# Expert loop: the down product of the preceding tile moved behind both gate and up pairs, the output copy behind both silus

## What is computed

```python
logits = x_flat @ gate_w.T
top_v, top_i = jax.lax.top_k(logits, 2)          # 2 of 8 experts for each token
hidden = silu(x_flat @ wge.T) * (x_flat @ wue.T)  # 512 hidden features
acc + we[:, None] * (hidden @ wde.T)
...
x = x + 0.5 * ffn(layernorm(x))
x = x + mamba(ln(x)) + mamba_reversed(ln(x))
x = x + 0.5 * ffn(layernorm(x))
```

## Time and profile before

| | us |
|---|---|
| median of 3 runs | 2637.85 (2635.95 to 2637.89) |
| span of the profiled execution | 2637.8 |
| PE, DVE, POOL, ACT busy | 2244.2, 2254.8, 2198.0, 1909.6 |
| the two expert loops in it | some 123 to 495 and 2222 to 2593 |

### The profile page before, as it was taken

The page is one execution under the profiler, slowest core; times in us unless marked ns, Lnnn a source line. Parts: engine busy times, 40 slices in busy tenths (PEclk is TensorE's granted clock), DMA queues, the critical chain, the costliest instruction groups (busy, mean ns, idle before and its releaser), DMA issues.

```text
span 2637.8 us, 49017 instructions
## 1 busy us (share of the span) xinstructions
PE 2244.2 (85%) x15840; PEld 1920.7 (73%) x15840; DVE 2254.8 (85%) x3430; ACT 1909.6 (72%) x3628; POOL 2198.0 (83%) x1402
## 2 busy tenths in 40 slices
PE   4899999768888898898898898988988768999992
PEld 3799999547676677777777676766777647999982
DVE  8766666789999999999999999999999897666666
ACT  4355555378998998998999899999898544555551
POOL 3577777369999999999999999999999936777771
PEclk8899999889999999999999999999999878999996
DMA  7011111433333333333333333333333240111116
GB/s 247 17 48 50 49 49 49 121 107 104 105 109 106 109 102 101 106 107 100 109 103 102 110 103 105 110 106 106 105 102 111 76 160 25 49 50 49 49 50 204
DMA packets 156813, 248.60 MB, mean 94 GB/s; under 512 B 22082, under 2 KB 66018, under 8 KB 155874
## 3 DMA queue, kind: packets, MB, share of 16 engines
q1 hardware_dynamic: 137568, 202.79, 25.9%
q0 software_dynamic: 18208, 37.26, 5.2%
q10 hardware_dynamic: 866, 6.43, 0.6%
HBM read 213.10 MB, written 33.29 MB: 93 GB/s over the span
## 4 chain that ended last, share of the span: by engine, by line
POOL 28%; PE 23%; issue 22%; DVE 14%; ACT 8%; DMA 4%; POOLq 0%; ACTq 0%; DVEq 0%; SPq 0%
POOL buf L484 10%; POOL buf L545 9%; DVE buf L914 6%; PE bank L1544 6%; POOL token_outputs L494 5%; PE bank L1419 4%; DMA buf<-state_rows 3%; PE bank L1329 3%; PE bank L1519 3%; POOL buf L532 2%; DVE buf L901 2%; ACT scaled L1194 2%; ACT over L1161 2%; DVE bank L886 2%; PE bank L1348 2%
## 5 line engine op out<-in xcount | busy, mean ns | idle before, releaser
L545 POOL TENSOR_TENSOR buf<-buf 128x1024 f32<-128x1024 f32 x512 | 1199.9, 2378 | 33.8 <-PE bank L1544 28.9
L914 DVE TENSOR_TENSOR_SCAN buf<-over,bank 128x512 f32<-128x512 f32 x832 | 953.6, 1198 | 5.2 <-PE bank L1519 2.6
L1161 ACT ACTIVATE over<-wgu,negA 128x510 f32<-128x510 f32 x832 | 541.2, 710 | 39.6 <-DVE buf L914 28.5
L1544 PE MATMUL bank<-id_sb,buf 128*128 128x128 f32 x4096 | 521.8, 282 | 6.3 <-POOL buf L545 6.3
L1544 PEld LDWEIGHTS bank<-id_sb,buf 128*128 128x128 f32 x4096 | 483.9, 146 | 55.8 <-issue 46.5
L1348 PE MATMUL bank<-parts 128*128 128x256 f32 x3408 | 480.3, 291 | 3.3 <-DVE buf L764 1.9
L1348 PEld LDWEIGHTS bank<-parts 128*128 128x128 f32 x3408 | 428.8, 192 | 7.2 <-issue 4.1
L1194 ACT ACTIVATE scaled<-wd_sb,I 128x256 f32<-128x256 f32 x896 | 377.3, 498 | 22.3 <-PE bank L1519 22.2
L494 POOL DMA_INDIRECT token_outputs<-buf,slot_out x284 | 287.7, 1013 | 111.1 <-issue 83.2
L484 POOL DMA_INDIRECT buf<-token_rows,slot_token x284 | 297.1, 1046 | 95.4 <-issue 89.7
L1519 PE MATMUL bank<-id_sb,scaled 128*128 128x128 f32 x1792 | 257.2, 281 | 91.3 <-ACT scaled L1194 40.8
(11 more groups left out here) (170 smaller groups left out, 2978.0 us busy)
## 6 DMA issues: line engine op xcount, KB each, us to landing
buf<-state_rows SPq DMA_DIRECT2D x608, 256.0 KB, 3.2
token_rows<-buf SPq DMA_DIRECT2D x32, 256.0 KB, 2.3
wd_sb<-token_outputs SPq DMA_DIRECT2D x16, 512.0 KB, 4.1
buf<-token_outputs SPq DMA_DIRECT2D x16, 512.0 KB, 4.9
buf<-token_rows,slot_token POOLq DMA_INDIRECT x284, 2.6
token_outputs<-buf,slot_out POOLq DMA_INDIRECT x284, 2.3
out<-X SPq DMA_DIRECT2D x16, 256.0 KB, 3.8
wgu<-wgT ACTq DMA_DIRECT2D x1, 2048.0 KB, 8.1
```

The lines of the kernel that those rows point to most:

```text
L545: pool.tensor_tensor(hC[:, b, :].rearrange("p (c w) -> p c w", c=C), hs[:, b, :].rearrange("p (c w) -> p c w", c=C), Cs[:, b, :].unsqueeze ...
L914: V.tensor_tensor_scan(hs[:, b, w], dA[:, b, c, :, :].rearrange("p s t -> p (s t)"), source, 0.0, ALU.mult, ALU.add).then_inc(s[f"scan_don ...
L1161: ins = A.activation(dA[:, n % R, c, :, 1:], delta[r][:, c * W:(c + 1) * W].rearrange("p (s t) -> p s t", s=S)[:, :, 1:], ACT.Exp, scale=n ...
L1544: ins = M.matmul(bank[4 + q // 2][:, at:at + P], hC[:, n % R, c * W + q * P:c * W + (q + 1) * P], id_sb[:, :], is_transpose=True, start=Fa ...
```

## The change

On PE `down(i-1)` moves from between the two halves of tile i to behind `up(i,1)`. On ACT `copy_out(i-1)` moves from between the two silus to behind `silu(i,1)`. Nothing is added or taken away. It applies to every tile but the first, in both mixtures of experts.

```diff
@@ ACT, four() @@
                         silu(i, 0)
+                        silu(i, 1)
                         if not (isinstance(i, int) and i == 0):
                             copy_out(i - 1, (q - 1) % 4, k if q else k - 1)
-                        silu(i, 1)
@@ PE, four() @@
                         gate(i, q % 2, 0)
                         up(i, q % 2, 0)
+                        gate(i, q % 2, 1)
+                        up(i, q % 2, 1)
                         if not (isinstance(i, int) and i == 0):
                             down(i - 1, (q - 1) % 2, (q - 1) % 4)
-                        gate(i, q % 2, 1)
-                        up(i, q % 2, 1)
```

## The result

| | before | after |
|---|---|---|
| median of 7 runs, us | 2637.89 (2635.95 to 2639.8) | 2647.51 (2644.11 to 2649.35) |
| span of the profiled execution, us | 2637.8 | 2642.8 |
| first scatter of each loop, us behind the loop's first gather | 19.2, 19.1 | 20.2, 20.5 |
| POOL's pace, 1st to 67th scatter, us a tile | 5.355, 5.342 | 5.432, 5.367 |
| first transfer of the 67th to that of the 71st scatter, us | 16.4, 16.6 | 16.4, 16.1 |

The changed kernel is slower: ratio 1.0034, 95% interval 1.0023 to 1.0045. The medians differ by 9.6 us, the two profiled executions by 5.0: a run's time is some 2 us above the span of the same execution (2644.9 against 2642.8 after), so the profiled execution before, with a span of 2637.8, was one of its slowest (some 2639.8 us, an estimate), and that of after was the second fastest of seven.

What follows compares the result with a forecast made beforehand. POOL's indirect transfers were taken to bound the expert loops at 5.35 us a tile; 2637.8 us plus 2.8 for later stream starts, 0 for the loop ends and 0 for the hold gave 2641 us, range 2629 to 2652.

Steps and rivals of the forecast that it cites:

- rival B: Expert loops: late `copy_out` drags `high_x` and L764, second gather held longer; pace 5.43, +13 us, 2651 us; chance 0.28.
- What bounds the loop: Expert loops: POOL's four indirect transfers a tile bound it, 5.15 us undisturbed, about 5.35 with the hold; PE needs 4.86.
- rival D: Expert loops: new order does more harm, for instance PE waiting for weights; pace 5.6, +36 us, 2674 us; chance 0.03.
- The output copy: ACT, each tile: `copy_out` comes 1.42 us later, 5.25 us after the transposes instead of 3.83.
- Start of the stream: POOL's first scatter waits for the first `copy_out`, so its stream starts 1.4 us later a loop, +2.8 us in all.
- End of the loop: Last tiles: back-to-back `down` gains some 0.8 us, the later last scatter loses 0.6 to 0.8; sum 0, within 0.8.
- ACT's queue: Reading the expert's number after `copy_out` takes 0.75 us, making `high_x` 0.1 us late, 0.4 in one of four tiles.
- What the hold becomes: POOL's second gather: three tiles of 5.40 us and one of 5.20 make 5.35, no change; bounds +11 and -26 us.
- The edge: POOL's second gather: a copy L764 0.4 us late starts after the gather is through; that tile costs 5.15 to 5.25.
- The named cause: DVE's weight copy L764 keeps POOL from descriptor work until 0.3 us after its start, adding 0.20 us a tile.
- the circle: Mid-loop: transposes to L764 3.34 us, to second gather's release 0.32, to next transposes 1.75; 5.41 us, 5.35 in the mean.
- The prediction's objection: POOL is released 0.3 us after L764's start, though its record runs 0.57; holding to its end would give 5.66 us a tile.

Runs made afterwards that it cites:

- the third: The changed kernel run a third time without edit, against the kernel before: ratio 1.0032 (1.0018 to 1.0046), pace 5.445 and 5.370 us.
- two_input_old: The kernel before with DVE's weight copy L764 written as the maximum of the weights with themselves, against the kernel before: ratio 1.0000, pace 5.357 us.

## Why the prediction was right and where it was wrong

The measured 2647.5 us lies inside the range, but nearer to rival B (2651) than to the forecast of 2641, and the change is clearly slower, to which I gave 0.35, where the likeliest case said no change (0.50). The range held because B was in it; what B says (the late `high_x` makes the hold longer) is what the first loop shows.

1. What bounds the loop: right. POOL stays without gaps, and every microsecond lost in the loop is a longer transfer or a later start. PE waits neither for weights nor for hidden values in the middle of the loops, so rival D is out.
2. The output copy: said 5.25 us behind the transposes, measured 5.18 (168.31 - 163.13).
3. Start of the stream: said +1.4 us a loop. Measured 1.0 and 1.4 in the first profile, 1.6 and 1.6 in the third.
4. End of the loop: said 0. From the 67th to the last scatter 16.43 us before, 16.44 after, in the first loop; 16.59 and 16.09 in the second.
5. ACT's queue: said 0.75 us from the output copy's start to `high_x` at the earliest. Measured 0.78 here (164.04 - 163.26), 0.79 in most of the quick tiles and 0.91 in the median. The first 0.38 us of it are the output copy itself; the idle time behind it is 0.40. The delay was real, and the run that reads the number first took it away: there the quickest tiles need 0.28 us.
6. What the hold becomes: this is the term that was mis-sized. I set a quarter of the tiles to escape the hold and the others at 5.40, so that the pace stayed at 5.35; it became 5.432 and 5.367, on average +0.05 us, and 132 x 0.05 = 6.7 us, which with the later start of 2.5 us makes 9.2 us. That this is near the 9.6 of the medians is partly luck, since the profiled executions differ by only 5.0: the stretch between the loops gave back 3.7 us and the end of the second loop 0.5. The share of free tiles was not what failed: of 58 tiles in the middle of each loop 16 and 30 have a second gather stretched by less than 0.05 us. But 10 and 13 had one before as well, so that the pace of 5.35 from which I counted already held some escapes, and I counted them once more. And the held ones grew by more than my 0.05 us: from 0.19 and 0.17 us in the mean to 0.31 and 0.29. In the first loop the longer holds win; in the second the many free tiles nearly make up for them. The edge is where the first subtraction starts together with the gather: a transfer that starts 0.07 us behind it is held for 0.46 us (165.69 against 165.62), one that starts within 0.03 us is not (the rows at 160.51).

The named cause was off by an instruction or two. The copy L764 starts 0.52 us behind the end of the first subtraction and 0.08 us ahead of the end of the second, and the rows I had could not part them; the distances I used (0.32 and 0.95 us from the copy's start) are 0.84 us from the end of the first and 0.87 us from the end of the second. Since all three move with `high_x`, the arithmetic of the circle was not harmed, but the experiment built on the wrong name (two_input_old) gained nothing where 20 to 27 us were expected. The prediction's objection, that the trace does not agree with a hold up to the instruction's end, falls with the name: measured from the right instruction, the hold lasts to its end.

The rule of the Trainium skill that I set beside it (SBUF — State Buffer, Who interferes with whom) names copies in a two-port mode. The same section of the Trainium skill also says that a DVE instruction with two inputs in SBUF contends with a GpSimd instruction that reads SBUF. That second sentence is the one that fits most of the holds: the subtractions have two such inputs, the indirect transfers take their row numbers from SBUF, and the trace agrees: with the copy on ACT 128 of 131 stretched transfers end 0.81 to 0.88 us after the end of one of them.

No run at the faster level beat the kernel before.

## What to carry to other kernels

An engine's register loads and branches are part of its queue's order: an instruction that waits late, put ahead of them, pushes their time (0.40 us here) onto the path of the next step, though the engine itself has idle time. When an engine off the chain shifts a step by 0.3 us, ask which other engine shares something with that step. Before blaming one of several neighbouring instructions, move one away from the others; where they can't be moved apart, look at what starts just ahead of each and just behind it, since a fixed distance to one is a fixed distance to all.

## What was not expected

- A subtraction on DVE with two inputs in SBUF delays an indirect transfer on POOL by up to 0.5 us, but only if the subtraction has started first, by some 0.05 us. If the transfer starts first, it is free, and the subtraction takes 0.71 us in the mean instead of 0.69. So a step that comes 0.3 us later can turn a hold of 0.2 us into one of 0.5 us or into none.
- The same kernel takes 2638 us in some comparisons and 2794 to 2816 us in others, with PE's products broken off for about 1 us in places and no releaser in the trace. The change is 0.3% slower at the first level and 0.5% faster at the second (ratio 0.9930 to 0.9965). What makes the level, the chip or something else, stays open.
